# A causal convolution as three half-width products, and score comparisons one step sooner

## The reference

```python
xz = x @ W_in                                   # 256 -> 512
xc, r = jnp.split(xz, 2, axis=-1)
xconv = conv_general_dilated(xc^T, conv_w, ...)  # 4 taps, causal, 256 x 256 channels
xs = xconv + conv_b
u = silu(xs)
delta = softplus((u @ W_x)[..., :128] @ W_dt + b_dt)
h = exp(delta * A) * h + delta * u * B           # scan over the tokens, 16 states per channel
y = sum_n(h * C) + u * D
x = layernorm(x + (y * silu(r)) @ W_out + xs)
scores = x @ w_router                            # the 64 best of 512 tokens, per sequence
x = layernorm(x + block(x of the chosen tokens, set back in place))
```

## Time and profile before

| | us |
|---|---|
| median of 3 runs | 475.49 (475.44 to 476.93) |
| the profiled execution | 474.69 |
| its span in the trace | 473.0 |
| first scan | 60.33 |
| first scan of step 16, 32, 48 | 126.33, 200.22, 271.49 |
| PE busy | 409.7 |
| DVE busy | 299.8 |
| ACT busy | 297.4 |
| POOL busy | 266.7 |

### The profile page before, as it was taken

The page is one execution under the profiler, slowest core; times in us unless marked ns, Lnnn a source line. Parts: engine busy times, 40 slices in busy tenths (PEclk is TensorE's granted clock), DMA queues, the critical chain, the costliest instruction groups (busy, mean ns, idle before and its releaser), DMA issues. The chain is left out here.

```text
span 473.0 us, 6478 instructions
## 1 busy us (share of the span) xinstructions
PE 409.7 (87%) x2037; PEld 248.9 (53%) x2037; DVE 299.8 (63%) x607; ACT 297.4 (63%) x631; POOL 266.7 (56%) x236
## 2 busy tenths in 40 slices
PE   5997899889999989999978789768978999999991
PEld 4442453344446435545434446334765867888880
DVE  0400664469583579865559977999488596554355
ACT  4225689797777697578699586963352565543152
POOL 2001056859688859779776989977553344331022
PEclk9998999999999989999989999978988999999996
DMA  7100611004210002410000515870500000000013
GB/s 238 49 0 21 162 48 43 22 22 116 89 46 22 22 24 51 111 44 22 24 22 14 148 40 165 240 289 1 179 0 2 0 1 1 3 1 0 1 56 122
DMA packets 18709, 29.10 MB, mean 62 GB/s; under 512 B 2698, under 2 KB 10676, under 8 KB 18420
## 3 DMA queue, kind: packets, MB, share of 16 engines
q1 hardware_dynamic: 18676, 28.70, 19.8%
HBM read 22.27 MB, written 2.23 MB: 52 GB/s over the span
## 5 line engine op out<-in xcount | busy, mean ns | idle before, releaser
L1189 DVE TENSOR_TENSOR_SCAN state<-front_a,bank 128x512 f32<-128x512 f32 x88 | 102.7, 1205 | 42.5 <-PE bank L538 21.3
L538 PEld LDWEIGHTS bank<-ident,loop_buf 128*128 128x128 f32 x512 | 59.6, 145 | 84.1 <-issue 34.9
L538 PE MATMUL bank<-ident,loop_buf 128*128 128x128 f32 x512 | 84.8, 288 | 18.2 <-ACT loop_buf L1030 17.7
L1040 ACT ACTIVATE front_a<-loop_buf,a_neg 128x512 f32<-128x512 f32 x128 | 84.1, 712 | 7.2 <-DVE copy L1189 4.6
L1030 ACT ACTIVATE loop_buf<-copy,b_rows 128x256 f32<-128x256 f32 x190 | 79.0, 496 | 0.1
L1564 POOL TENSOR_TENSOR state<-state,front_a 128x1024 f32<-128x1024 f32 x22 | 54.2, 2464 | 21.7 <-DVE state L1189 16.7
L554 PE MATMUL bank<-front_c,conv_raw 128*128 128x512 f32 x128 | 59.2, 594 | 2.5 <-ACT front_c L902 0.9
L1189 DVE TENSOR_TENSOR_SCAN copy<-front_a,bank 128x512 f32<-128x512 f32 x40 | 46.8, 1207 | 20.6 <-ACT front_a L1040 7.7
L1564 POOL TENSOR_TENSOR state<-state,c_own 128x1024 f32<-128x1024 f32 x22 | 52.3, 2380 | 4.4 <-DVE state L1189 4.0
L675 PE MATMUL bank<-state,fold 128*64 128x512 f32 x176 | 50.1, 647 | 0.8 <-POOL state L1564 0.8
L1577 POOL TENSOR_TENSOR loop_buf<-copy,b_rows 128x512 f32<-128x512 f32 x31 | 33.5, 1081 | 28.6 <-ACT copy L902 26.0
(11 more groups left out here) (201 smaller groups left out, 726.5 us busy)
## 6 DMA issues: line engine op xcount, KB each, us to landing
front_a<-c_stage SPq DMA_DIRECT2D x32, 128.0 KB, 2.9
c_own<-c_stage SPq DMA_DIRECT2D x32, 128.0 KB, 2.9
loop_buf<-front_b SPq DMA_DIRECT2D x32, 128.0 KB, 2.3
copy<-in_L_attn_x SPq DMA_DIRECT2D x4, 512.0 KB, 3.7
front_b<-in_L_ffn_wo SPq DMA_DIRECT2D x1, 2048.0 KB, 10.0
copy<-in_L_ffn_wq SPq DMA_DIRECT2D x1, 2048.0 KB, 8.1
out<-loop_buf SPq DMA_DIRECT2D x3, 512.0 KB, 3.0
conv_raw<-in_L_attn_conv_w SPq DMA_DIRECT2D x2, 512.0 KB, 3.8
```

What stands on the lines that cost most here:

```text
L538: return pe.transpose(dst, src, ident[:])
L1040: act.activation(decay[:, u % NDA, :], delta_wide[:, b % 2, k, :], ACT.Exp, scale=a_neg[:, k, m:m + 1]).then_inc(decay_made, 1)
L1189: dve.tensor_tensor_scan(state[t % NH][:, j, :], decay[:, u % NDA, :], bank[BU_BANK[u % NBU]][:], 0.0, ALU.mult, ALU.add).then_inc(scanned, 1)
```

## The change

With even and odd columns apart, the output is

- even[s] = w0 x[2s] + w2 x[2s+2], for 257 values of s,
- odd[s] = w1 x[2s+1] + w3 x[2s+3], for 256,
- y[2s] = even[s] + odd[s],
- y[2s+1] = (w0+w1)(x[2s+1] + x[2s+2]) + (w2+w3)(x[2s+3] + x[2s+4]) - even[s+1] - odd[s].

Three products of two taps over half of the columns take the place of four taps over all. Piece a makes *even* in a bank of its own, b makes *odd* in the left half of `cv`, c the third product in its right half; d has no matmul. `even` and `odd` read `xT` at every second column. The sums of the taps (`add_taps`) and of neighbouring columns (`x_pair`, one operation for each batch, placed at `xT1` in DVE's queue) are made by DVE. ACT copies *even* to SBUF in the steps of a. The last additions and the bias are three DVE operations in the steps of d, where ACT's copy is gone; `su` waits for them. The other part moves `k0`, `k1` to step 11, `k2`, `k3` to 12, `pf` to 13, `ga` and `cs` to 14.

```diff
@@ -52,8 +52,8 @@
 FIRST_BU = ("cv0c", "cv0d")
 TAIL_AT = {
     2: ("y0", "y1", "g0", "g1"), 4: ("o0",), 5: ("o1",), 6: ("ls0", "ls1"), 7: ("lp0", "lp1"),
-    8: ("la0", "la1"), 9: ("lx0", "lx1"), 10: ("sb",), 11: ("k0",), 12: ("k1",), 13: ("k2", "k3"),
-    14: ("pf",), 15: ("ga", "cs"),
+    8: ("la0", "la1"), 9: ("lx0", "lx1"), 10: ("sb",), 11: ("k0", "k1"), 12: ("k2", "k3"),
+    13: ("pf",), 14: ("ga", "cs"),
 }
 
 
@@ -126,6 +126,8 @@
                 continue
             if piece[:2] == "cv":
                 if piece[-1] == "a":
+                    add_rest(("even" + piece[2], b))
+                elif piece[-1] == "b":
                     held[0] = add_rest((piece[:3], b))
                 elif piece[-1] == "d":
                     held[0] = None
@@ -314,6 +316,9 @@
 
         gT_buf = sb("gT", [P, KD * L])
         gT = gT_buf[:].rearrange("p (k l) -> p k l", k=KD)
+        HALF = L // 2
+        even_buf = gT_buf[:, 0:KD * (HALF + 1)].rearrange("p (k s) -> p k s", k=KD)
+        odd_part = gT_buf[:, KD * (HALF + 1):KD * (HALF + 1) + HALF]
         z = sb("z", [P, C, DM])
         compared = z[:].rearrange("p c d -> p (c d)").bitcast(BF16).rearrange("p (c j) -> p c j", c=C)
         stats = sb("stats", [P, C, 6])
@@ -331,6 +336,8 @@
         place = sb("place", [P, C])
         onehot = sb("onehot", [P, B // 2, C, 2 * K])
         sel = sb("sel", [P, ST, NCOL])
+        tap_sum = h_buf[:].rearrange("p (m k o) -> p m k o", m=TAPS // 2, k=KD)
+        x_pair = change_buf[:].rearrange("p (k s) -> p k s", k=KD)
         cosT = sb("cosT", [P, S])
         sinT = sb("sinT", [P, S])
 
@@ -378,6 +385,8 @@
         dve_seq = sem("dve_seq")
         act_seq = sem("act_seq")
         pool_seq = sem("pool_seq")
+        x_paired = sem("x_paired")
+        taps_added = sem("taps_added")
         u_ready = sem("u_ready")
         silu_ready = sem("silu_ready")
         res_ready = sem("res_ready")
@@ -539,21 +548,39 @@
 
             pe.wait_ge(consts, 1)
 
-            def convolve(b, o, quarter):
-
-                name = (f"cv{o}", b)
-                if quarter == 0:
+            def convolve(b, o, part):
+                out = slice(o * P, (o + 1) * P)
+                wait_drained(pe, ("xT0", b))
+                wait_drained(pe, ("xT1", b))
+                if part == "a":
+                    name = (f"even{o}", b)
                     wait_free(pe, name)
-                    wait_drained(pe, ("xT0", b))
-                    wait_drained(pe, ("xT1", b))
                     pe.wait_ge(conv_pad, 1)
-                for j in range(2 * quarter, 2 * quarter + 2):
-                    k, i = j // KD, j % KD
+                    for j in range(2 * KD):
+                        m, i = j // KD, j % KD
+                        if b == 0:
+                            wait_drained(pe, ("vc", 2 * i + m))
+                        mm = pe.matmul(at(name)[:, 0:HALF + 1], conv_x[:, 2 * m, i, out], xT[:, i, 2 * m:2 * m + L + 1:2],
+                                       start=(j == 0), stop=(j == 2 * KD - 1))
+                    fill_done(name, mm)
+                elif part == "b":
+                    name = (f"cv{o}", b)
+                    wait_free(pe, name)
+                    for j in range(2 * KD):
+                        m, i = j // KD, j % KD
+                        mm = pe.matmul(at(name)[:, 0:HALF], conv_x[:, 2 * m + 1, i, out], xT[:, i, 2 * m + 1:2 * m + L:2],
+                                       start=(j == 0), stop=(j == 2 * KD - 1))
+                elif part == "c":
+                    name = (f"cv{o}", b)
+                    pe.wait_ge(x_paired, b + 1)
                     if b == 0:
-                        wait_drained(pe, ("vc", 2 * i + k // 2))
-                    mm = pe.matmul(at(name)[:], conv_x[:, k, i, o * P:(o + 1) * P], xT[:, i, k:k + L],
-                                   start=(j == 0), stop=(j == TAPS * KD - 1))
-                if quarter == 3:
+                        pe.wait_ge(taps_added, 4)
+                    for i in range(KD):
+                        mm = pe.matmul(at(name)[:, HALF:], tap_sum[:, 1, i, out], x_pair[:, i, :],
+                                       start=(i == 0), stop=(i == KD - 1), skip_group_check=True)
+                    for i in range(KD):
+                        mm = pe.matmul(at(name)[:, HALF + 1:], tap_sum[:, 0, i, out], x_pair[:, i, 0:HALF - 1],
+                                       start=False, stop=True, skip_group_check=True)
                     fill_done(name, mm)
 
             def front(b, piece):
@@ -562,7 +589,7 @@
                 if piece in NO_FILL:
                     return
                 if piece[:2] == "cv":
-                    return convolve(b, int(piece[2]), "abcd".index(piece[3]))
+                    return convolve(b, int(piece[2]), piece[3])
                 wait_free(pe, name)
                 t = at(name)
                 if piece in ("xT0", "xT1"):
@@ -920,18 +947,17 @@
                     copy_out(name, silu_r[b % 2][:, o, :], func=ACT.Silu)
                     if o == 1:
                         act.preload_act_table_set("natural_log_exp_and_others")
-                elif piece in ("cv0d", "cv1d"):
+                elif piece in ("cv0a", "cv1a"):
                     o = int(piece[2])
-                    if b == 0 and o == 0:
-                        wait_drained(act, "vec")
                     if b >= 1:
-                        act.wait_ge(res_ready, b)
-                    copy_out((piece[:3], b), xsT[:, o, :], func=ACT.Identity, bias=vec[:, CB + o:CB + o + 1])
+                        wait_drained(act, (f"cv{o}", b - 1))
+                    copy_out((f"even{o}", b), even_buf[:, o, :], at((f"even{o}", b))[:, 0:HALF + 1])
                     if b == 0 and o == 0:
 
                         act.preload_act_table_set("silu_and_others")
                         rope_tables()
                 elif piece == "su":
+                    wait_drained(act, ("cv0", b))
                     wait_drained(act, ("cv1", b))
                     if b >= 2:
                         act.wait_ge(y_taken, KD * (b - 1))
@@ -1095,6 +1121,7 @@
                     front(1, "xT0")
                     front(1, "xT1")
                 front(0, piece)
+            front(1, "cv0a")
             front(0, "du0")
             front(0, "du1")
             make_z(0, 0)
@@ -1102,7 +1129,7 @@
             act.wait_ge(a_ready, 2)
             make_decay(0)
             make_decay(1)
-            front(1, "cv0d")
+            front(1, "cv1a")
             for t in range(B * NST):
                 for u in range(2 * t + 2, min(2 * t + 4, NU)):
                     make_decay(u)
@@ -1198,8 +1225,40 @@
                     dve.tensor_scalar(zed[:, 0, c, :, i, :], du_rows[0][:, c, :].rearrange("p (k d) -> p k d", k=2 * KD), b_rows[:, 0, c, i:i + 1], None,
                                       ALU.mult).then_inc(z_dve, 1)
 
+            def add_taps():
+
+                for v in range(4):
+                    j, k = v // 2, 2 * (v % 2)
+                    wait_drained(dve, ("vc", v))
+                    dve.tensor_tensor(tap_sum[:, k // 2, j, :], conv_x[:, k, j, :], conv_x[:, k + 1, j, :],
+                                      ALU.add).then_inc(taps_added, 1)
+
             def front(b, piece):
-                if piece == "s3" and b == 0:
+                if piece == "xT1":
+                    wait_drained(dve, ("xT0", b))
+                    wait_drained(dve, ("xT1", b))
+                    if b == 0:
+                        dve.wait_ge(conv_pad, 1)
+                    dve.tensor_tensor(x_pair, xT[:, :, PAD:PAD + L - 1:2], xT[:, :, PAD + 1:PAD + L:2], ALU.add)\
+                        .then_inc(x_paired, 1)
+                elif piece in ("cv0d", "cv1d"):
+                    o = int(piece[2])
+                    name, t = (f"cv{o}", b), at((f"cv{o}", b))
+                    wait_drained(dve, (f"even{o}", b))
+                    wait_filled(dve, name)
+                    if b == 0 and o == 0:
+                        wait_drained(dve, "vec")
+                    if b >= 1:
+                        dve.wait_ge(res_ready, b)
+                        dve.wait_ge(u_ready, b)
+                    cols = xsT[:, o, :].rearrange("p (s e) -> p e s", e=2)
+                    shift_by = vec[:, CB + o:CB + o + 1]
+                    dve.scalar_tensor_tensor(out=cols[:, 0], in0=t[:, 0:HALF], scalar=shift_by, in1=even_buf[:, o, 0:HALF],
+                                             op0=ALU.add, op1=ALU.add)
+                    link(dve.tensor_tensor(odd_part, t[:, 0:HALF], even_buf[:, o, 1:], ALU.add))
+                    drain_done(name, dve.scalar_tensor_tensor(out=cols[:, 1], in0=t[:, HALF:], scalar=shift_by, in1=odd_part,
+                                                              op0=ALU.add, op1=ALU.subtract))
+                elif piece == "s3" and b == 0:
 
                     for h in range(KD):
```

(4 more changed lines are left out.)

## The result

The changed kernel takes **489.52 us** in the median of 4 runs (488.64 to 490.48), the kernel before on the same chip 475.83 us (475.44 to 476.93): ratio **1.029, 95% interval 1.025 to 1.034**. The forecast was 469.7 us with a range of 465.5 to 475.5, so it was wrong in size and in sign. The profiled execution took 490.08 us. Medians in this document are over all runs of a kernel; the ratios and their intervals leave out runs in a slower state of the chip, in which the same kernel takes longer.

A forecast was written before the change was run, and what follows sets the result against it. TensorE was taken to set the pace beside the convolution, VectorE in steps without it. Terms -2.8 - 1.1 - 2.3 + 1.2 - 0.8 = -5.8 us, from a median of 475.49, gave 469.7 us, range 465.5 to 475.5.

The forecast's parts named there:

- An operation of four results can be slowed beside POOL: Steps 24 to 33: operations slowed beside POOL were the main spread; chosen took 1.66 us, one on as many results 0.17.
- 0.3 to 1.8 for the count: Step 29: DVE time allowed for the count, in us, before pf could start at about 193.
- steps 40 to 48: Stretch without convolution: comparisons release their bank sooner, gather and tables leave the step where scan 97 waits; -0.8 us.
- The weighing of the contention rule: DVE operations with two SBUF inputs contend with GpSimd; pair sums lose 0.2 us in step 8, nothing in step 24.
- PE hardly notices, with four banks to fill ahead: Steps 24 to 33: the batch 3 pair sum delays scan 52 to 179.3 to 180.1 from 175.84, with little effect on PE.
- the bound of +3: Steps 24 to 33: upper bound in us on the predicted sum of +1.2 at step 34; the lower was -1.
- rival B: DVE's queue becomes the bound: pair-sum waits (+2.0, +4.0) and two drains stay in full; 480.2 us, chance 0.10.
- Steps 0 to 7, -1.1: Batch 1's convolution: SiLU starts some 2.0 us sooner, but PE ends r1's product only 1.1 us sooner; -1.1 us.
- The prologue, -2.8: Before the loop: the product ends 3.45 us sooner and the drain takes 0.6 more; -2.8 us.
- the term of 10.4 us for one batch's product: New convolution of one batch on PE: 48 records of 0.217 us, 10.4 us against 13.8 for the old.
- rival C: Operand read at every second column runs at half rate, 0.430 us a record; 486 us, chance 0.06.
- Steps 8 to 17, -2.3: Batch 2's convolution: less PE work and ACT waiting, against DVE 2.0 us late from the pair sum; -2.3 us.

The follow-up runs named there:

- the table alone: The kernel before with only the choice's pieces moved (comparisons to steps 11 and 12, places 13, gather and tables 14): 484.03 us, ratio 1.015.
- the late pair sum: The changed kernel with the neighbour sums of x made one step later from batch 2 on: 484.30 us, ratio 1.017.
- the short *chosen: Here: changed kernel with old step order, even1 in the other bank, later neighbour sums, no offset, chosen writing an accumulator: 468.63 us, ratio 0.989.

## Why the prediction was wrong

**"An operation of four results can be slowed beside POOL" was seen and mis-sized.** The step that failed for the table is the spread of "0.3 to 1.8 for the count", added to a start of pf at 193 and to nothing else. It counted *chosen*, 1.66 us before, and left out *offset*, which follows it and runs into POOL's next operation: 3.8 us together, twice (1.52 + 2.27), against 1.8 and 2.6 us in the kernel before. For steps 40 to 48 the prediction counted no such cost at all and wrote -0.8; it was +6.0 in the trace, +5.4 with the table alone. In the row before, 1.66 us was a harmless figure, since a wait for PE followed. The move took that cover away, and the prediction had not named what hid it. It saw that PE would stand until *chosen* is made, and gave that wait no price beyond the late start of `pf`; that the clock would be at half for 10.3 us behind it stands nowhere in the sum. The weighing of the contention rule stopped at the pair sums. The operations of *chosen* and *offset* and the router products come under the same page. The Trainium skill (SBUF — State Buffer, Who interferes with whom) says more than was used: a tensor_scalar can run in a mode with both pairs of ports, except in the form that also writes its accumulator; a tensor_reduce never contends; two SBUF inputs contend with a GpSimd operation that reads SBUF; and who comes second waits for the whole instruction. The runs agree: tensor_scalar held 1.52 and 2.27 us, with the accumulator 0.16, tensor_reduce 0.17, two SBUF inputs 1.50 and 2.57. They add that the wait can be for more than one instruction (6.18 us above).

**Steps 24 to 33: "PE hardly notices, with four banks to fill ahead" and the bound of +3 failed.** Scan 52 was put at 179.3 to 180.1 and came at 182.84, with 1.7 of that from the stretch's late start. The wait itself was right in place and cause (6.94 us, some 7 forecast). What was missing is the router product held beside POOL, 2.2 us. The convolution alone cost +6.9 us here, of which the late pair sum takes back 5.3 (with the short *chosen* too, 1.0 is left), so rival B's mechanism (the pair sum's wait in full in steps 24 to 33, where DVE is the limit) was the true one. Its price for steps 8 to 17 was not.

**Steps 0 to 7, -1.1: the step "ACT copies nothing there, so that SiLU starts some 2.0 us sooner" looked at the wrong piece.** The drain's move to DVE was costed by its duration (1.3 us) and as a delay of what follows it. Not costed was that the bank it frees now comes free behind two scans, and that the next fill goes to the same bank. +4.8 us; with the other bank -1.5 against the kernel before.

**The prologue, -2.8: the mechanism held, and the size was -2.2.** The product in the trace of the change:

```profile
22.28 2.06 PE L563 MATMUL bank<-front_c,conv_raw 128*128 128x257 f32 x8 [0.73 <-ACT front_c L929]
24.18 1.98 PE L571 MATMUL bank<-front_c,conv_raw 128*128 128x256 f32 x8
26.00 1.02 PE L579 MATMUL bank<-change,h 128*128 128x256 f32 x4
...
27.72 1.98 PE L563 MATMUL bank<-front_c,conv_raw 128*128 128x257 f32 x8
29.54 1.99 PE L571 MATMUL bank<-front_c,conv_raw 128*128 128x256 f32 x8
31.37 1.02 PE L579 MATMUL bank<-change,h 128*128 128x256 f32 x4
32.23 1.02 PE L582 MATMUL bank<-change,h 128*128 128x255 f32 x4
```

The strided records come (29.54 - 27.72) / 8 = 0.2275 and (31.37 - 29.54) / 8 = 0.229 us apart, the contiguous ones (27.72 - 26.00) / 8 = 0.215. (The very first group shows 0.2375, because its first interval is 0.304.) So the term of 10.4 us for one batch's product was 10.8 (22.28 to 33.25, less the tail of the last record), and rival C (0.430) is refuted. The product lasts 10.97 us instead of 13.98, 3.0 us less where 3.45 were counted, and the drain ends 1.4 us behind it (at 34.69) instead of 0.7. From the start of the product to the first scan it is 39.1 us in all seven traces with the old product and 36.7 to 36.9 in all seven with the new one: -2.2 us. That the first scan of this trace came only 1.1 us sooner is due to the start, 22.28 instead of 21.24. That start is not the change's doing: it lies between 19.4 and 22.6 us with either product.

**Steps 8 to 17, -2.3, was -1.1:** the wait for the pair sum (4.97 us) and its absorption by PE were right. What was missing is probably clock: PE ran at 0.50 from 104.4 to 107.8, and in the kernel before at full clock throughout; every trace with the new convolution has at least such a stretch there, and only one with the old. By the rows of the last section such a stretch costs about 1.3 us here (an estimate), which is the difference. Why the new convolution meets half clock there is open. **Steps 18 to 23 and 34 to 39** were left out and gave 0.9 us each, with the table alone nothing; so it is the convolution.

The forecast of -5.8 had gains of about the right kind in the prologue and in steps 8 to 17; with the 0.9 us twice that nobody had forecast they made about -4 us in this trace. Under them lay three costs: +4.5 (a bank), +8.7 (mostly the pair sum), +6.0 (the held operations and what follows from them). The chances are also added up wrongly: by the prediction's own shares faster is 0.76 and slower 0.14, not 0.78 and 0.12.
